# Running the two pairs of a triangular inverse in different rounds, with projection products between the steps

## The chip, the cores and the metric

The kernel runs on one core of a Trainium2 chip. TensorE does the matrix products and transpositions, VectorE (DVE), ScalarE (ACT) and GpSimd (POOL) the work around them, and SyncE (SP) issues most transfers. Each engine runs its own instructions strictly in order and waits on semaphores for the others. The metric is the device time of the whole kernel in microseconds: the median of several runs.

## The reference, cut to what matters

The program is two layers. The change touches the first, a gated delta rule over 8 sequences of 1024 steps with a 128x128 state each:

```python
q = x @ Wq + bq;  v = x @ Wv + bv;  gate = sigmoid(x @ Wg + bg)
kr = x @ Wk + bk; k = kr / max(norm(kr), 1e-12)
alpha = sigmoid(x @ Wa + ba);  beta = sigmoid(x @ Wb + bb)
# per step and sequence
Sk = S @ k_t
S  = a * (S - b * outer(Sk, k_t)) + b * outer(v_t, k_t)
o  = (q_t @ S) * g_t
x  = layernorm(x + o @ Wo + bo)
```

After it come a quantised MLP of six matrices with LoRA parts and a low rank MLP, each with a LayerNorm. Their code is the same in both kernels.

## The kernel before, in words

The 128 steps of a chunk are solved at once. Within a chunk the rule is a triangular system, so each chunk and sequence needs the inverse of a unit triangular 128x128 matrix. There are 8 chunks, and the 8 sequences go in two groups of four: 16 **rounds** of four sequences. A round belongs to one chunk and one group.

In a round, for the sequences s = 0 to 3: `xT.s` transposes the input (four 128x128 transpositions on TensorE, a rounded copy on ScalarE, the rest of the rounding on VectorE); `seed` writes the bias into a PSUM bank on ScalarE; `proj.s` is 12 products of 512 columns (four slices of the input, three products each, since every fp32 value is split in a high and a low part); `sq` and `copy` take q, k, v and the gate out on ScalarE. `ab`, `decay` and `A` make the decays of alpha and beta; `root` and `kh` norm k; `qkT` transposes q and k; `kk` multiplies k with itself; `MnT`, `M`, `W0` make the first state of the inverse.

The **levels** follow. The inverse is built by doubling: six levels, each for two **pairs** of sequences (pair 0 is s = 0, 1 and pair 1 is s = 2, 3). A level i of pair h is: `T.i.h` transposes the state (2 transpositions, then a copy on ScalarE into `Z_both`), `Y.i.h` multiplies it with M (then VectorE copies a masked part into `L`), `X.i.h` multiplies Z with L (then VectorE adds into the state `XZ`). The sixth ends in `inverse`. The chain of a level is TensorE, VectorE, TensorE, VectorE, and the next level of the same pair needs its end. The two pairs alternate, so one fills part of the other's waits.

With the inverse made, the round's second half runs a round later (a `'` in the order), mixed with the next round's first half: `KS`, `U`, `PT`, `O`, `S` compute the outputs and the new state, `ogT` and `attn.s` the output projection, and `z`, `stats`, `norm` the residual and LayerNorm. `''` is two rounds later.

The order is written out by hand, in the text `ORDER`, which the same function `run` reads for each engine: an engine takes from it the pieces in which it has work. The loop body holds two rounds. The last round has an order with more pieces (`MORE`, `ORDER_LAST`), among them the unpacking of the quantised weights (`dequant`) for the next layer, and `TAIL` follows. PSUM has eight banks, and the names `p_tr`, `p_pj`, `p_small`, `p_wide`, `p_pair` say which piece writes where.

## Time and profile before

| what | value |
|---|---|
| median of 3 runs | 2498.21 us (2495.07 to 2499.21) |
| profiled execution | 2494.1 us, its span 2492.3 us |
| busy over the span | PE 97%, DVE 67%, ACT 47%, POOL 27% |
| first layer's rounds | from 8.6 us to 722.5 us of the span |
| a round in the steady state | 43.2 us |

PE is TensorE, PEld its weight loads. A row of the timeline is a start, a duration, an engine, a line of the code, what is written and read, and in brackets how long the engine had been idle and for whom. A small product's duration is mostly latency: 128 columns take 0.27 us from start to end, but the next starts 0.11 us after it. So the busy share of PE says little about how full it is, and the distances between starts are used instead.

### The profile page before, as it was taken

The numbers are of one execution on the slowest core, as the hardware profiler recorded it, in microseconds if no ns is written. First come the engines' busy times: TensorE is split into PE (matmuls) and PEld (weight loads), VectorE is DVE, ScalarE is ACT, GpSimd is POOL, SyncE is SP. The second block draws the span as 40 slices with busy tenths as digits, with TensorE's granted clock in tenths as the row PEclk, the third lists the DMA queues.
The fourth block names the chain that finished last, engine by engine and source line by source line (L and its number), as shares of the span: only waits on it lengthen the run. The fifth ranks groups of instructions, "written<-read, shape, count | busy, mean of one in ns | idle before, by whom it ended". The sixth has DMA issues, their size and how long they took to land.

```text
span 2492.3 us, 37474 instructions
## 1 busy us (share of the span) xinstructions
...
## 2 busy tenths in 40 slices
...
GB/s 132 52 68 40 94 67 101 34 101 67 77 140 59 1 68 35 17 84 0 83 18 17 84 0 101 0 17 84 0 101 46 75 95 102 106 114 121 113 84 68
DMA packets 100655, 166.28 MB, mean 67 GB/s; under 512 B 18356, under 2 KB 21428, under 8 KB 100468
## 3 DMA queue, kind: packets, MB, share of 16 engines
...
q10 hardware_dynamic: 4036, 1.84, 0.3%
...
## 4 chain that ended last, share of the span: by engine, by line
PE 66%; DVE 1%; POOL 1%; issue 0%; ACT 0%; POOLq 0%; DVEq 0%
PE quant_bank L1436 7%; PE quant_bank L1438 7%; PE quant_bank L1437 7%; PE quant_bank L1826 6%; PE quant_bank L1828 6%; PE quant_bank L1827 6%; PE quant_bank L1463 5%; PE quant_bank L1464 5%; PE quant_bank L1465 5%; PE quant_bank L1453 3%; PE quant_bank L1482 2%; PE quant_bank L1484 2%; PE quant_bank L1483 2%; PE quant_bank L1843 1%; PE quant_bank L1494 1%; PE quant_bank L1425 1%
## 5 line engine op out<-in xcount | busy, mean ns | idle before, releaser
L1305 ACT ACTIVATE quant_g_hi<-quant_bank,kept_beta,kept_gamma 128x512 fp32r<-128x512 f32 x192 | 150.6, 784 | 395.6 <-PE quant_bank L1453 395.6
L1277 POOL TENSOR_SCALAR quant_var<-quant_mv 128x1 f32<-128x1 f32 x256 | 56.9, 222 | 1006.2 <-DVE quant_mv L1352 1006.2
L1436 PE MATMUL quant_bank<-kept_W_hi,quant_h_hi 128*128 128x512 f32 x768 | 305.4, 398 | 0.3 <-DVE quant_h_lo L1341 0.3
L1437 PE MATMUL quant_bank<-kept_W_lo,quant_h_hi 128*128 128x512 f32 x768 | 303.5, 395 | 0.0
L1438 PE MATMUL quant_bank<-kept_W_hi,quant_h_lo 128*128 128x512 f32 x768 | 303.4, 395 | 0.0
L1350 DVE BATCH_NORM_STATS2 quant_stats<-quant_bank 128x6 f32<-128x512 f32 x192 | 133.9, 698 | 196.4 <-PE quant_bank L1438 196.4
L1791 DVE TENSOR_TENSOR mlp_g_lo<-quant_bank,mlp_g_hi 128x512 fp32r<-128x512 f32 x256 | 176.4, 689 | 105.4 <-ACT quant_bank L1728 105.3
L1727 ACT ACTIVATE mlp_g_hi<-quant_bank,mlp_b 128x512 fp32r<-128x512 f32 x256 | 177.3, 693 | 70.7 <-PE quant_bank L1828 63.6
L1463 PE MATMUL quant_bank<-quant_g_hi,kept_W_hi 128*128 128x512 f32 x512 | 205.2, 401 | 0.0
L1464 PE MATMUL quant_bank<-quant_g_hi,kept_W_lo 128*128 128x512 f32 x512 | 202.5, 396 | 0.0
L1465 PE MATMUL quant_bank<-quant_g_lo,kept_W_hi 128*128 128x512 f32 x512 | 202.4, 395 | 0.0
L1372 DVE TENSOR_TENSOR quant_g_lo<-quant_bank,quant_g_hi 128x512 fp32r<-128x512 f32 x192 | 130.2, 689 | 100.4 <-ACT quant_bank L1306 98.2
L1320 ACT ACTIVATE quant_bank<-kept_b_all 128x512 f32<-128x512 f32 x192 | 113.3, 603 | 133.3 <-DVE quant_y L1365 74.7
L1438 PEld LDWEIGHTS quant_bank<-kept_W_hi,quant_h_lo 128*128 128x128 f32 x768 | 144.0, 187 | 35.1
L1436 PEld LDWEIGHTS quant_bank<-kept_W_hi,quant_h_hi 128*128 128x128 f32 x768 | 144.0, 188 | 34.6 <-issue 0.5
L1437 PEld LDWEIGHTS quant_bank<-kept_W_lo,quant_h_hi 128*128 128x128 f32 x768 | 144.1, 188 | 34.1
L1728 ACT ACTIVATE quant_bank<-quant_bank,mlp_b 128x512 f32<-128x512 f32 x256 | 168.3, 658 | 0.0
L1365 DVE TENSOR_SCALAR quant_y<-quant_bank,quant_mv,quant_rstd 128x512 f32<-128x512 f32 x192 | 155.5, 810 | 17.2 <-POOL quant_rstd L1279 17.2
L1279 POOL TENSOR_TENSOR quant_rstd<-quant_var,quant_minus_half 128x1 f32<-128x1 f32 x256 | 140.9, 550 | 21.3
L1306 ACT ACTIVATE quant_bank<-quant_bank,kept_beta,kept_gamma 128x512 f32<-128x512 f32 x192 | 145.4, 757 | 0.0
L1315 ACT ACTIVATE quant_h_hi<-kept_x_in 128x512 fp32r<-128x512 f32 x128 | 81.9, 640 | 123.6 <-DVE kept_x_in L1384 99.7
L1686 POOL TENSOR_SCALAR mlp_z<-mlp_z,mlp_mv,mlp_rstd 128x512 f32<-128x512 f32 x60 | 123.9, 2082 | 0.0
...
## 6 DMA issues: line engine op xcount, KB each, us to landing
...
```

Source lines behind the costliest of these rows:

```text
L1305: nc.scalar.activation(g_hi[m][:, k, :], tr[k][:, :], ACT.Gelu, bias=beta[:, b, k:k + 1], scale=gamma[:, b, k:k + 1])
L1365: nc.vector.tensor_scalar(y[m][:, e, :], lin_of["up", m, b, e][:, :], mv[m][:, e, 0:1], rstd[m][:, e:e + 1], ALU.subtract, ALU.mult).then_ ...
L1436: mm(out, x_hi, W_hi[2 * b][:, k, :], start=False, stop=False, skip_group_check=True)
L1437: mm(out, x_hi, W_lo[2 * b][:, k, :], start=False, stop=False, skip_group_check=True)
L1438: last = mm(out, x_lo, W_hi[2 * b][:, k, :], start=False, stop=k == KT - 1, skip_group_check=True)
L1463: mm(out, W_hi[2 * b + 1][:, k, cols], g_hi[m][:, k, :], start=k == 0, stop=False)
L1464: mm(out, W_lo[2 * b + 1][:, k, cols], g_hi[m][:, k, :], start=False, stop=False)
L1465: last = mm(out, W_hi[2 * b + 1][:, k, cols], g_lo[m][:, k, :], start=False, stop=k == KT - 1)
L1727: nc.scalar.activation(g_hi[:, at, :], p_h[at][:, :], ACT.Gelu_apprx_tanh, bias=b1[:, f:f + 1])
L1728: nc.scalar.activation(p_h[at][:, :], p_h[at][:, :], ACT.Gelu_apprx_tanh, bias=b1[:, f:f + 1]).then_inc(s_["gelu_done"], 1)
L1791: nc.vector.tensor_tensor(g_lo[:, at, :], p_h[at][:, :], as_f32(g_hi[:, at, :]), ALU.subtract).then_inc(s_["g_lo_done"], 1)
L1826: mm(out, lhs[0], rhs[0], start=first, stop=False)
```

## The change

The two pairs no longer alternate. Pair 0's levels stay at the end of the round, pair 1's move to the start of the next one, where they carry a `'`. Between the products of a level stand other pieces: the projections, cut into six parts each (`proj.s.0` to `proj.s.3` are two products, the high input against both parts of the weights; `proj.s.4` and `.5` are two products with the low input), and `xT`, `KS`, `PT`, `O`, `ogT`. `Y` now comes ahead of `T`. `seed` is a piece of its own. `S` is cut in four and the state update `Su` is put behind it; `PT` and `O` are cut in two and four. The state update and the four residual additions on GpSimd (`res`) get places of their own. Each pair gets its own semaphores and two banks in place of shared ones. In the last round pair 1's levels follow alone, since there is no next round, and the unpacking of the weights is spread over pair 0's levels. The number of products, transpositions and copies in a round is the same.

```diff
-        kk_halves = [p[:, 0:2 * P].rearrange("p (s n) -> p s n", s=2) for p in (p_small, p_tr[0])]
-
+        kk_halves = [p_tr[0][:, 0:2 * P].rearrange("p (s n) -> p s n", s=2)] * 2
+        YX_bank, T_bank = [p_tr[0], p_pair[1]], [p_tr[1], p_small]
...
-        Y_ps_of = [p_wide[:, 0:P], p_tr[1][:, 0:P]]
-        X_ps_of = [p[:, 0:P] for p in p_pair]
-        last_ps_of = [p[:, 0:P].rearrange("p (y n) -> p y n", y=2) for p in p_pair]
+        Y_ps_of = [p[:, 0:P] for p in YX_bank]
+        X_ps_of = [p[:, P:2 * P] for p in YX_bank]
+        last_ps_of = [p[:, 2 * P:3 * P].rearrange("p (y n) -> p y n", y=2) for p in YX_bank]
+        T_halves = [p[:, 0:2 * P].rearrange("p (s n) -> p s n", s=2) for p in T_bank]
...
         ORDER = order("""
-            bv.0' xT.0 xT.1 KS.0' proj.0 stats.0'' stats.1'' stats.2'' sq.0 copy.0 U.0' xT.2 proj.1 norm.0'' stats.3'' norm.1'' sq.1 copy.1 PT.0' xT.3 norm.2'' norm.3''
-            S.0' O.0' ab.0 root.0 proj.2 sq.2 copy.2 ogT.0' decay.0 kh.0
-            proj.3 sq.3 root.1 qkT.0 qkT.1 copy.3 attn.0' A.0 kh.1 kk.0 attn.1' MnT.0 qkT.2 qkT.3 qkA.0 z.0' M.0 W0.0 attn.2' z.1' kk.1 attn.3' MnT.1 M.1 W0.1
-            T.1.0 Y.1.0 T.1.1 Y.1.1 X.1.0 X.1.1
-            T.2.0 Y.2.0 T.2.1 Y.2.1 X.2.0 X.2.1
-            T.3.0 Y.3.0 T.3.1 Y.3.1 X.3.0 X.3.1
-            T.4.0 Y.4.0 T.4.1 Y.4.1 X.4.0 X.4.1
-            T.5.0 Y.5.0 T.5.1 Y.5.1 X.5.0 X.5.1
-            T.6.0 Y.6.0 T.6.1 Y.6.1 inverse.0 z.2' inverse.1 z.3'""")
+            bv.0' xT.0 seed.0 xT.1 seed.1
+            Y.1.1' T.1.1' proj.0.0 stats.0'' X.1.1' proj.0.1
+            Y.2.1' T.2.1' proj.0.2 stats.1'' X.2.1' proj.0.3 xT.2
+            Y.3.1' T.3.1' proj.0.4 norm.0'' X.3.1' proj.0.5 sq.0 copy.0 seed.2 stats.2''
+            Y.4.1' T.4.1' proj.1.0 norm.1'' X.4.1' proj.1.1 xT.3
+            Y.5.1' T.5.1' proj.1.2 stats.3'' X.5.1' KS.0'
+            Y.6.1' T.6.1' proj.1.3 norm.2'' inverse.1' proj.1.4 proj.1.5 sq.1 copy.1 seed.3
+            ab.0 norm.3'' root.0 U.0' proj.2.0 proj.2.1 decay.0 kh.0 proj.2.2 proj.2.3 S.0' S.1' qkT.0 qkT.1 A.0 S.2' kk.0 S.3' MnT.0 res.0' proj.2.4 proj.2.5 sq.2 copy.2 M.0 W0.0
+            Y.1.0 T.1.0 PT.0' X.1.0 PT.1'
+            Y.2.0 T.2.0 O.0' X.2.0 O.1' res.1'
+            Y.3.0 T.3.0 O.2' X.3.0 O.3' res.2'
+            Y.4.0 T.4.0 proj.3.0 X.4.0 proj.3.1 res.3'
+            Y.5.0 T.5.0 proj.3.2 Su.0' X.5.0 proj.3.3 Su.1'
+            Y.6.0 T.6.0 proj.3.4 Su.2' ogT.0' inverse.0 Su.3' proj.3.5 sq.3 copy.3 root.1
+            attn.0' kh.1 attn.1' z.0' qkT.2 attn.2' qkT.3 kk.1 attn.3' z.1' MnT.1 M.1 W0.1 z.2' z.3' qkA.0""")
...
+        MORE = {("KS", 0, 1): [("unit", 0, 0)] + dequants((0, 0)),
+                ("ab", 0, 0): dequants((0, 1), (0, 2), (0, 3)),
+                ("kh", 0, 0): dequants((1, 0), (1, 1)),
+                ("kh", 1, 0): [("bv", 0, 0)]}
+        for i, tiles in enumerate(([(1, 2)], [(1, 3)], [(2, 0)], [(2, 1)], [(2, 2), (2, 3)])):
+            MORE["X", (i + 1, 0), 0] = dequants(*tiles)
...
+        for i in range(1, LEVELS - 1):
+            ORDER_LAST += [("Y", (i, 1), 0), ("T", (i, 1), 0)]
+            if i < 5:
+                ORDER_LAST += [("stats", i - 1, 1)]
+            ORDER_LAST += [("X", (i, 1), 0)]
+            if i > 1:
+                ORDER_LAST += [("la_hi", i - 2, 0), ("norm", i - 2, 1)]
+        ORDER_LAST += [("Y", (LEVELS - 1, 1), 0), ("T", (LEVELS - 1, 1), 0), ("lb_hi", 0, 0), ("inverse", 1, 0), ("lb_hi", 1, 0), ("lb_hi", 2, 0)]
...
-                seed(c, g, s)
...
+            def proj(c, g, at):
+
+                s, part = at
+                n = GROUPS * c + g
+                if part == 0:
+                    if isinstance(n, int) and n == s == 0:
+                        pe.wait_ge(s_["w_lo_done"], 2)
+                    pe.wait_ge(s_["xT_hi_done"], GB * n + s + 1)
+                    pe.wait_ge(s_["seeded"], GB * n + s + 1)
+                if part == KT:
+                    pe.wait_ge(s_["xT_lo_done"], GB * n + s + 1)
                 out, cols = p_pj[s % 2][:, :], slice(0, PROJ)
-                for k in range(KT):
-                    mm(out, xT_hi[:, s, k, :], w_hi[:, k, cols], start=False, stop=False, skip_group_check=True)
-                    mm(out, xT_hi[:, s, k, :], w_lo[:, k, cols], start=False, stop=False, skip_group_check=True)
-                pe.wait_ge(s_["xT_lo_done"], GB * n + s + 1)
-                for k in range(KT):
-                    last = mm(out, xT_lo[:, s, k, :], w_hi[:, k, cols], start=False, stop=k == KT - 1, skip_group_check=True)
-                last.then_inc(s_["proj_ps"], 1)
+                if part < KT:
+                    mm(out, xT_hi[:, s, part, :], w_hi[:, part, cols], start=False, stop=False, skip_group_check=True)
+                    mm(out, xT_hi[:, s, part, :], w_lo[:, part, cols], start=False, stop=False, skip_group_check=True)
+                else:
+                    for k in (2 * (part - KT), 2 * (part - KT) + 1):
+                        last = mm(out, xT_lo[:, s, k, :], w_hi[:, k, cols], start=False, stop=k == KT - 1, skip_group_check=True)
+                    if part == KT + 1:
+                        last.then_inc(s_["proj_ps"], 1)
...
+            def PT_(c, g, h):
+
+                if h == 1:
+                    dve.wait_ge(s_["PT_ps"], GROUPS * c + g + 1)
+                    nc.vector.tensor_tensor(PT[:, :, :], wide, DT[g][:, :, :], ALU.mult).then_inc(s_["PT_done"], 1)
...
+            def Su(c, g, s):
+
+                n = GROUPS * c + g
+                if s == 0:
+                    dve.wait_ge(s_["O_ps"], n + 1)
+                dve.wait_ge(s_["S_ps"], 2 * n + s // 2 + 1)
+                nc.vector.scalar_tensor_tensor(S[g][:, s, :, :], S[g][:, s, :, :], A[g][:, s, P - 1:P], pair[s // 2][:, s % 2, :, :],
+                                               ALU.mult, ALU.add).then_inc(s_["S_done"], 1)
...
+                if s == 2:
+                    pe.wait_ge(s_["inverse_done"], 2 * n + 1)
...
+                nc.tensor.transpose(T_halves[h][:, 1, :], MnT[:, 2 * h + 1, :], ident).then_inc(s_["M_ps"], 1)
```

TensorE, one level in the steady state, in the order of the kernel before (both pairs; p_small and p_wide are pair 0's banks, p_tr pair 1's):

```order
L923 MATMUL delta_p_small<-kept_ident_61,delta_XZ_114 128x128
L924 MATMUL delta_p_small<-kept_ident_61,delta_XZ_114 128x128
L933 MATMUL delta_p_wide<-delta_XZ_114,delta_M_both 128x128
L923 MATMUL delta_p_tr<-kept_ident_61,delta_XZ_114 128x128
L924 MATMUL delta_p_tr<-kept_ident_61,delta_XZ_114 128x128
L933 MATMUL delta_p_tr<-delta_XZ_114,delta_M_both 128x128
L941 MATMUL delta_p_pair<-delta_L_81,delta_Z_both 128x128 x2
```

and in the changed order, the second level of pair 1 (L956 is Y, L944 and L945 are T, L859 and L860 projection products, L964 is X, L843 transposes the input of the third sequence):

```order
L956 MATMUL delta_p_pair<-delta_XZ_114,delta_M_both 128x128
L944 MATMUL delta_p_small<-kept_ident_61,delta_XZ_114 128x128
L945 MATMUL delta_p_small<-kept_ident_61,delta_XZ_114 128x128
L859 MATMUL delta_p_pj<-delta_w_hi,delta_xT_hi 128x512
L860 MATMUL delta_p_pj<-delta_w_lo,delta_xT_hi 128x512
L962 REGISTER_ALU
L964 MATMUL delta_p_pair<-delta_L_79,delta_Z_both 128x128
L859 MATMUL delta_p_pj<-delta_w_hi,delta_xT_hi 128x512
L860 MATMUL delta_p_pj<-delta_w_lo,delta_xT_hi 128x512
L843 MATMUL delta_p_tr<-kept_ident_61,delta_x_in_110 128x128 x4
```

The other pair's products are gone from the level, and products of a projection stand in both gaps.

TensorE, from the last projection's end on, before (L889 is qkT of the first two sequences, L1017 to L1019 attn, L897 is kk):

```order
L845 MATMUL delta_p_pj<-delta_w_hi,delta_xT_lo 128x512 x4
L889 MATMUL delta_p_tr<-kept_ident_61,delta_qkv 128x128
L889 MATMUL delta_p_tr<-kept_ident_61,delta_kb 128x128
L889 MATMUL delta_p_tr<-kept_ident_61,delta_khat_69 128x128
L889 MATMUL delta_p_tr<-kept_ident_61,delta_qkv 128x128
L889 MATMUL delta_p_tr<-kept_ident_61,delta_kb 128x128
L889 MATMUL delta_p_tr<-kept_ident_61,delta_khat_69 128x128
L1017 MATMUL delta_p_pj<-delta_wo_hi,delta_ogT_hi 128x512
L1018 MATMUL delta_p_pj<-delta_wo_lo,delta_ogT_hi 128x512
L1019 MATMUL delta_p_pj<-delta_wo_hi,delta_ogT_lo 128x512
L897 MATMUL delta_p_small<-delta_qkT_75 128x128 x2
```

and now (L1051 to L1053 attn, L910 qkT of the third sequence):

```order
L863 MATMUL delta_p_pj<-delta_w_hi,delta_xT_lo 128x512 x2
L1051 MATMUL delta_p_pj<-delta_wo_hi,delta_ogT_hi 128x512
L1052 MATMUL delta_p_pj<-delta_wo_lo,delta_ogT_hi 128x512
L1053 MATMUL delta_p_pj<-delta_wo_hi,delta_ogT_lo 128x512
L1051 MATMUL delta_p_pj<-delta_wo_hi,delta_ogT_hi 128x512
L1052 MATMUL delta_p_pj<-delta_wo_lo,delta_ogT_hi 128x512
L1053 MATMUL delta_p_pj<-delta_wo_hi,delta_ogT_lo 128x512
L910 MATMUL delta_p_tr<-kept_ident_61,delta_qkv 128x128
L910 MATMUL delta_p_tr<-kept_ident_61,delta_kb 128x128
L910 MATMUL delta_p_tr<-kept_ident_61,delta_khat_103 128x128
L1051 MATMUL delta_p_pj<-delta_wo_hi,delta_ogT_hi 128x512
L1052 MATMUL delta_p_pj<-delta_wo_lo,delta_ogT_hi 128x512
```

The transpositions of the first two sequences have left the place between the last projection and attn, and two attn stand ahead of the third sequence's.

VectorE, from the second pair's first state on, before (L704 to L708 are W0, L714 the masked copies of both pairs' first level, L720 the addition):

```order
L704 COPY_PREDICATED delta_XZ_76<-delta_mask_both,delta_MnT 128x64
L706 COPY_PREDICATED delta_XZ_76<-delta_mask_both,delta_p_tr 128x64
L708 TENSOR_TENSOR delta_M_both<-delta_p_pair,delta_MnT 128x128
L39 ISA
L714 COPY_PREDICATED delta_L_78<-delta_mask_both,delta_p_wide 128x128
L39 REGISTER_ALU
L714 COPY_PREDICATED delta_L_78<-delta_mask_both,delta_p_tr 128x128
```

and now (L713 and L715 are W0, L781 is z, L685 bv, L644 the low part of xT, L721 the masked copy of pair 1's first level):

```order
L713 COPY_PREDICATED delta_XZ_76<-delta_mask_both,delta_p_small 128x64
L715 TENSOR_TENSOR delta_M_both<-delta_p_small,delta_MnT 128x128
L780 REGISTER_ALU
L781 TENSOR_TENSOR delta_z<-delta_p_pj,delta_x_res_123 128x512 x2
L685 TENSOR_TENSOR delta_bv_70<-delta_qkv,delta_ab 128x512
L643 ISA
L644 TENSOR_TENSOR delta_xT_lo<-delta_p_tr,delta_xT_hi 128x512
L643 REGISTER_ALU
L644 TENSOR_TENSOR delta_xT_lo<-delta_p_tr,delta_xT_hi 128x512
L721 COPY_PREDICATED delta_L_78<-delta_mask_both,delta_p_pair 128x128
```

Two z, bv and two low parts now stand between the first state and the first level's copy.

## Rows read from the trace of the kernel before

**Rows 1.** Stages: us, busy and instructions per engine, TensorE clock, DMA share, GB/s

```profile
405.70:448.87 43.17, 41.97 (x262) 34.39 (x262) 30.32 (x73) 16.25 (x46) 13.06 (x19) 1.00 0.28 97
435.94:448.87 12.93, 11.73 (x78) 9.43 (x77) 7.61 (x27) 3.54 (x12) 2.49 (x4) 1.00 0.00 0
```

**Rows 2.** Timeline of one level: start, us, engine, line, what; idle before in brackets

```profile
401.41 0.28 PE L923 MATMUL delta_p_small<-kept_ident,delta_XZ 128*128 128x128 f32 x1
401.64 0.39 PE L933 MATMUL delta_p_wide<-delta_XZ,delta_M_both 128*128 128x128 f32 x2
401.84 0.28 ACT L596 ACTIVATE delta_Z_both<-delta_p_small 128x128 f32<-128x128 f32 x1 [1.19 <-PE delta_p_small L924]
402.13 0.30 DVE L714 COPY_PREDICATED delta_L<-delta_mask_both,delta_p_wide 128x128 f32<-128x128 int32 x1 [0.23 <-PE delta_p_wide L933]
...
402.57 1.05 PE L941 MATMUL delta_p_pair<-delta_L,delta_Z_both 128*128 128x128 f32 x4
...
403.07 0.29 DVE L720 TENSOR_TENSOR delta_XZ<-delta_p_pair,delta_XZ 128x128 f32<-128x128 f32 x1
403.46 0.28 PE L923 MATMUL delta_p_small<-kept_ident,delta_XZ 128*128 128x128 f32 x1
```

**Rows 3.** Timeline: first projection, then U's eight products

```profile
407.57 0.47 PE L841 MATMUL delta_p_pj<-delta_w_hi,delta_xT_hi 128*128 128x512 f32 x1
...
410.43 0.28 PE L967 MATMUL delta_p_pair<-delta_XZ,delta_bR 128*128 128x128 f32 x1
...
411.32 0.28 PE L970 MATMUL delta_p_pair<-delta_bR,delta_XZ 128*128 128x128 f32 x1
```

**Rows 4.** Timeline: from the last projection to the third transposition of q and k

```profile
429.99 0.28 ACT L558 ACTIVATE delta_sq<-delta_p_pj 128x128 f32<-128x128 f32 x1 [3.36 <-PE delta_p_pj L845]
...
431.77 0.43 DVE L667 TENSOR_TENSOR delta_kb<-delta_qkv,delta_rnb 128x256 f32<-128x256 f32 x1
...
432.60 0.32 PE L889 MATMUL delta_p_tr<-kept_ident,delta_qkv 128*128 128x128 f32 x1
```

**Rows 5.** Timeline: second pair, from the product of k to its first state

```profile
434.13 2.38 POOL L494 TENSOR_TENSOR delta_qkA<-delta_qkT,delta_A 128x1024 f32<-128x1024 f32 x1 [2.52 <-ACT delta_qkT L584]
...
435.56 1.11 DVE L704 COPY_PREDICATED delta_XZ<-delta_mask_both,delta_MnT 128x64 f32<-128x64 int32 x1
...
436.52 0.30 DVE L706 COPY_PREDICATED delta_XZ<-delta_mask_both,delta_p_tr 128x64 f32<-128x64 int32 x1
```

**Rows 6.** Timeline: ScalarE and VectorE at a round's start

```profile
406.34 0.60 ACT L550 ACTIVATE delta_xT_hi<-delta_p_tr 128x512 fp32r<-128x512 f32 x1 [1.47 <-PE delta_p_tr L829]
...
406.40 0.68 DVE L767 TENSOR_TENSOR delta_z<-delta_p_pj,delta_x_res 128x512 f32<-128x512 f32 x1
...
406.83 0.60 ACT L545 ACTIVATE delta_p_pj<-delta_b_all 128x512 f32<-128x512 f32 x1
...
407.00 0.68 DVE L678 TENSOR_TENSOR delta_bv<-delta_qkv,delta_ab 128x512 f32<-128x512 f32 x1
```

**Rows 7.** Timeline: one LayerNorm statistic

```profile
409.40 0.69 DVE L772 BATCH_NORM_STATS2 delta_stats<-delta_z 128x6 f32<-128x512 f32 x1
```

**Rows 8.** Timeline: ScalarE behind a finished projection, first and last

```profile
415.64 0.28 ACT L558 ACTIVATE delta_sq<-delta_p_pj 128x128 f32<-128x128 f32 x1 [1.70 <-PE delta_p_pj L845]
...
416.28 0.28 ACT L563 ACTIVATE delta_gate<-delta_p_pj 128x128 f32<-128x128 f32 x1
```

**Rows 9.** Timeline: the products for alpha and beta, and their last sigmoid

```profile
420.26 0.48 PE L855 MATMUL delta_p_tr<-delta_xT_hi,delta_w_ab 128*34 128x512 f32 x1
...
424.36 0.70 ACT L571 ACTIVATE delta_a_rest<-delta_ab_sum,delta_b_ab 2x508 f32<-2x508 f32 x1
```

**Rows 10.** First round, a thinly filled stretch: columns as in rows 1

```profile
42.00:44.00 2.00, 0.89 (x7) 0.64 (x6) 2.00 (x5) 0.76 (x2) 0.00 (x0) 1.00 0.00 0
44.00:46.00 2.00, 1.43 (x7) 1.14 (x8) 1.24 (x5) 0.11 (x1) 1.81 (x1) 0.59 0.00 0
```

**Rows 11.** Last round, a stretch of waits: columns as in rows 1

```profile
690.00:700.00 10.00, 4.48 (x15) 3.44 (x14) 6.22 (x12) 0.60 (x3) 1.80 (x4) 0.67 0.86 279
```

169 lines of the change are left out of this document (78 added, 91 removed).

## The prediction

> **What bounds the kernel now.** I read the summary of engines first, then the stages of one round, then the timeline of a level and of the places where pieces change their neighbours. The change touches only the first layer, 16 rounds, so everything is worked out per round. A steady round takes 43.17 us, with VectorE busy for 30.32 us of it and ScalarE for 16.25 [rows 1]. The levels are its last 12.93 us. PE shows 11.73 us busy there, but that counts latency. By starts it is less full: a level of both pairs repeats every 2.05 us (401.41 to 403.46) [rows 2]. A small product or transposition issues every 0.11 us, so a level needs 4 transpositions (0.44), 2 Y and 2 X of two passes each (0.89), 1.33 us. Five levels and the sixth thus leave TensorE about 4.4 us without work per round. Outside the levels I find about 1 us. So TensorE's own work is about 38 us a round, and the prize is at most 5 us a round, 80 us in all. The bound inside the levels is a chain through three engines, outside it TensorE.
>
> **One pair alone.** With Y ahead of T, and from the handoffs of rows 2: Y at 0; T issues at 0.22; the copy on ScalarE starts 0.43 later (401.41 to 401.84) and takes 0.28; X starts 0.14 after a finished input (402.43 to 402.57), so at 1.07. The masked copy of Y starts at 0.49 (401.64 to 402.13) and ends at 0.79, so it is not late. The addition starts 0.50 after X (402.57 to 403.07), takes 0.29, and the next Y comes 0.10 later (403.36 to 403.46). Sum 1.96 us for **one** pair, against 2.05 for both before. The sixth level ends in two longer product groups, about 1.7. Two pairs: 10 x 1.96 + 2 x 1.7 = 23.0 us of chain, 10.1 more than 12.93.
>
> **What moves into it.** A projection takes 2.86 us of TensorE (407.57 to 410.43), a part 0.47; eight passes of 128 columns take 0.89 (410.43 to 411.32) [rows 3]. Into the gaps go proj.0 (2.86), four parts of proj.1 (1.9), five of proj.3 (2.4), KS and PT (0.89 each), O (1.78), xT.2 and xT.3 (0.44 each), ogT (0.44): 12.0 us. Were nothing else late, the round would be 43.2 + 10.1 - 12.0 = 41.3 us. That is 1.9 less than now, not the 5 of the prize, since a level has 1.30 us free and gets 0.94 to 1.4. What follows is what else becomes late. I worked it out by putting the pieces on the five engines in the new order with the durations of the rows.
>
> **The stretch from the last projection to pair 1's first X.** TensorE work in it: four attn (2.8), qkT.2 and .3 (0.66), kk.1 (0.45), M.1 (0.22), xT.0 and .1 (0.88), Y, T and a part (0.9), 5.9 us. The waits, one by one:
> a. attn.0' needs the low part of ogT: two operations of 0.60 and 0.69 us behind ogT, which stands just ahead of the end of the chain: 0.65.
> b. qkT.2 needs kh.1. From the square of the last projection to it the trace shows 2.61 us (429.99 to 432.60) [rows 4], through ScalarE, VectorE, GpSimd and back. Before, qkT.0, qkT.1, kk.0 and two attn covered this. Now two attn do (1.4 us), and the first VectorE step queues behind ogT_lo, an addition and a state update (0.9 more): 1.45.
> c. attn.2' needs z.0', which is queued behind kh.1 on VectorE: 0.35.
> d. kk.1 stands directly behind qkT.3 and waits for its copy on ScalarE: 0.8.
> e. The first state (W0.1) has a copy that starts at 435.56 and takes 1.11 us, and the next one, of 0.30, starts at 436.52, when the 2.38 us of GpSimd's qkA (from 434.13) end [rows 5]. qkA still starts with qkT.3's copy, so W0.1 ends no sooner, and Y.1.1' with it. xT.0 and xT.1 cover 0.9 of it, 0.6 is left. The Trainium skill says that GpSimd's memory interface is shared with VectorE and contended where VectorE has two SBUF inputs (GPSIMD Engine Reference, 1. Specifications); this trace agrees, and by that rule the residual additions, which now stand behind kh.0, could hold up W0.0 as well.
> f. The largest: before pair 1's first masked copy VectorE has z.2', z.3', bv, and the low parts of xT.0 and xT.1 to do. Such operations follow one another every 0.6 us (406.40 to 407.00) [rows 6], 3.0 us from W0.1's end. ScalarE's copy of T stands behind two high parts and two seeds, 0.5 us each (406.34 to 406.83), and ends before the masked copy does. So X.1.1' starts 3.4 us after Y.1.1' and not 1.07: 2.35.
> Sum 6.2 us, where the same pieces cost about 0.8 now: +5.4.
>
> **Pair 1's levels.** In level 3 the high and low part of xT.2 run ahead of the masked copy, and in level 5 those of xT.3: transpose, 0.3, ScalarE 0.60, VectorE 0.68, then the copy, so X is late by 0.9 each. In level 4 ScalarE does sq, copy, gate and seed of the first projection ahead of T's copy: 0.92 from sq to the gate's end (415.64 to 416.56) [rows 8], and 0.5 for the seed, started only when proj.0.5 has ended: X late by 0.9. The gaps of levels 2, 4 and 5 get more (1.11 to 1.13 us with X) than the 0.89 that the chain has there: 0.7. A statistic of 0.69 us and its follower stand ahead of the additions of levels 1 and 2 [rows 7], and KS's subtraction ahead of the sixth copy: 0.3. Sum 3.7.
>
> **Between the pairs.** From ab's first product to the end of the last sigmoid it is 4.8 us (420.26 to 425.06) [rows 9]. Then decay, a scan, kh.0, qkT, kk.0, MnT.0 and W0.0 follow in a chain, 13.0 us to Y.1.0 by the same handoffs. It holds 11.0 us of TensorE's work (ab 1.84, U 1.78, proj.2 2.86, decay 1.4, S 1.78, the rest 1.3). So 2.0 of waits, against about 0.5 now: +1.5.
> **Pair 0's levels.** PT's product on VectorE must end before O.0' may start, and og and Su stand ahead of copies: +0.4.
>
> Sum of a round: 41.3 + 5.4 + 3.7 + 1.5 + 0.4 = 52.3 us.
>
> **The clock.** In the first round TensorE was busy for 0.89 of 2 us, and in the next 2 us the granted clock was 0.59 on average [rows 10]: it fell from 2.4 to 1.2 GHz behind a stretch that was less than half filled. The wait f is such a stretch: in the 3.4 us from Y.1.1' to X.1.1' 0.9 us of work is issued. The work of the one or two levels behind it (1.3 to 1.6 us each) then issues at half rate, but partly in gaps of the chain. No row prices it: 0 at least, and up to 3 us a round. I take 0.7, nearer to nothing, since the steady rounds of rows 1, waits included, show a granted clock of 1.00. Round: 53.0 us, 9.8 more than now.
>
> **The ends.** Pair 1's levels of the last round run alone at the end: 5 x 1.96 + 1.7 = 11.5 us more. Against that, the last round waits today: in 690 to 700 us there is little work and the clock is low [rows 11], because six dequants that need late loads stand ahead of the chain. Now three of them do, and the others lie between the levels. That gives back 6 to 9 us, and the statistics and norms that come out of the tail some 3 more. The first round gains and loses alike. I count the ends at 0, within +-6.
>
> 15 rounds x 9.8 = +147 us on the profiled 2494.1 is 2641. The runs' median stands 4 us above the profiled execution: **2645 us**. With half of each contention term the round is 47 and the time 2555. With the clock's upper end it is 55.5 and 2680, with the waits a tenth longer 2695. Its own range is 2560 to 2700.
>
> **Rivals.**
> 1. *The chain covers what I count as late, faster.* If the VectorE queue at a round's start and ScalarE's block in level 4 ran inside waits that pair 1 has anyway, the round were 41.3 + about 0.8 of stalls, 42.1: 2498 - 15 x 1.1 - 6 = 2475 us. For it speaks that VectorE has 12.85 us of idle time a round and ScalarE 27. Against it: they work in order, and the pieces stand ahead of the level's copy in the new order, so idle time behind them doesn't help. It decides when a, b and f together are under 1 us; I find 4.5. 0.10, with 0.02 more for no difference.
> 2. *Half covered.* The overlaps of neighbouring operations hide more than I count, because durations contain latency: round 46, 2540 us. 0.12.
> 3. *The clock stays down.* If the stretches of waits b to f keep TensorE at 1.2 GHz into pair 1's levels, then some 7 us of products issue at half rate: +7 a round, 2645 + 15 x 6.3 = 2740 us. 0.08. The Trainium skill tells of kernels whose clock falls anew in each waiting gap and is paid for each time (TensorE: Matmul & The Clock Gate, HAM oscillation). By that rule this would be the likely case; the steady round here shows a granted clock of 1.00, and only the first and last rounds bear the rule out.
>
> **Chances.** The forecast 0.68, rival 2 0.12, rival 3 0.08, rival 1 0.12 with the tie. A measurement of this kernel tells 0.2% (5 us) from no change. Faster 0.10, same 0.02, slower 0.88. The range 2550 to 2700 leaves out the faster case, part of rival 2 and most of rival 3.
>
> **What would show it.** Rounds 53 us apart by the starts of xT.0. VectorE's z and bv rows directly ahead of pair 1's first masked copy, and X.1.1' 3 to 3.5 us behind Y.1.1' (f). About 1.5 us of idle TensorE ahead of qkT.2, waiting for khat (b). In pair 1's third, fourth and fifth level X about 2 us after Y, in the others 1.1. Pair 0's levels 1.95 to 2.1 us apart. A granted clock below 1 at the round's start, if the clock's term is real. It would be wrong if the rounds are 42 us apart with a full TensorE, or if one pair's level takes less than 1.8 us.

## The result: slower by 7.0%

| kernel | median | ratio to before, 95% interval | span of the profiled execution |
|---|---|---|---|
| before | 2496.93 us | | 2492.3 us |
| changed | 2671.64 us | 1.0702 [1.0687, 1.0717] | 2669.0 us |

The prediction was 2645 us with a range of 2550 to 2700. The time lies in the range, 27 us above the value named.

The profile page of the changed kernel, its busy shares and granted clock (tenths, 40 slices):

```profile
PE 2463.2 (92%) x12383; PEld 1956.2 (73%) x12383; DVE 1688.8 (63%) x3181; ACT 1173.2 (44%) x2225; POOL 670.6 (25%) x1090
PEclk7999999999999899999999999999999999999999
```

The profiled execution takes 177 us more for the same work and every share is lower: time went into waits. Stretches of the changed kernel, columns as in [rows 1]:

```profile
390.42:445.33 54.91, 45.11 (x263) 33.74 (x261) 31.31 (x73) 16.50 (x46) 13.59 (x20) 0.97 0.22 76
449.78:465.69 15.91, 13.39 (x73) 10.36 (x73) 9.26 (x25) 3.90 (x12) 3.22 (x8) 0.91 0.00 0
885.00:900.00 15.00, 10.13 (x37) 6.71 (x37) 10.05 (x26) 2.78 (x8) 6.95 (x10) 0.66 0.35 56
```

The first is a whole steady round (xT.0 to xT.0), which answers to the first line of [rows 1]: 54.9 us for 43.17, with 45.1 us of TensorE busy for 42.0, since latency and a lower clock count as busy. The mean of 14 rounds is 54.50 us against 43.22. The second reaches from X.1.1' to ab's first product and holds the rest of pair 1's levels; the third is the end of the last round, where pair 1's levels stand alone.

**Wait f, the largest.** Timeline of the changed kernel from pair 1's first Y to its first X:

```profile
446.36 1.27 DVE L781 TENSOR_TENSOR delta_z<-delta_p_pj,delta_x_res 128x512 f32<-128x512 f32 x2
447.55 0.68 DVE L685 TENSOR_TENSOR delta_bv<-delta_qkv,delta_ab 128x512 f32<-128x512 f32 x1
448.15 1.28 DVE L644 TENSOR_TENSOR delta_xT_lo<-delta_p_tr,delta_xT_hi 128x512 fp32r<-128x512 f32 x2
446.68 0.50 PE L956 MATMUL delta_p_pair<-delta_XZ,delta_M_both 128*128 128x128 f32 x2 [0.26 <-DVE delta_M_both L715]
449.35 0.29 DVE L721 COPY_PREDICATED delta_L<-delta_mask_both,delta_p_pair 128x128 f32<-128x128 int32 x1
449.78 0.55 PE L964 MATMUL delta_p_pair<-delta_L,delta_Z_both 128*128 128x128 f32 x1 [1.26 <-DVE delta_L L721]
```

Y starts at 446.68, X at 449.78, 3.10 us later. By the handoff of [rows 2] the masked copy that X needs (L721) could start 0.49 us behind Y, yet five operations stand ahead of it on VectorE, and it starts 2.67 us behind. X follows its end.

**The clock behind it.** Windows of 2 us of the changed kernel:

```profile
448.00:450.00 2.00, 0.74 (x3) 0.33 (x3) 2.00 (x5) 0.86 (x3) 0.00 (x0) 0.83 0.00 0
450.00:452.00 2.00, 2.00 (x9) 1.75 (x9) 0.76 (x4) 0.00 (x0) 0.75 (x2) 0.50 0.00 0
452.00:454.00 2.00, 2.00 (x13) 1.64 (x12) 1.30 (x4) 0.28 (x1) 0.73 (x2) 0.81 0.00 0
```

TensorE is busy for 0.74 of 2 us, and then it runs at 1.2 GHz (0.50), as in [rows 10]. By windows of 1 us the granted clock is 0.67 from 449 to 450, 0.50 to 452, 0.63 to 453 and 1.00 from there on.

**Where the sum was short.** VectorE and GpSimd of the changed kernel between the pairs, and the first transposition of q and k:

```profile
418.58 0.90 DVE L674 TENSOR_TENSOR delta_kb<-delta_qkv,delta_rnb 128x256 f32<-128x256 f32 x1
419.40 1.48 DVE L675 TENSOR_TENSOR delta_khat<-delta_qkv,delta_rn 128x256 f32<-128x256 f32 x1
416.69 5.33 POOL L520 TENSOR_TENSOR delta_x_res<-delta_x_res,delta_bo_all 128x512 f32<-128x512 f32 x4
421.01 0.32 PE L910 MATMUL delta_p_tr<-kept_ident,delta_qkv 128*128 128x128 f32 x1 [1.66 <-DVE delta_khat L675]
```

In [rows 4] kb takes 0.43 us. Here it takes 0.90 and khat 1.48, beside four residual additions on GpSimd, and TensorE waits 1.66 us for khat.

### The profile page after: what moved, and what is told of

Its sections match the earlier page's. It is cut to its first block, busy times and chain, and to the rows that moved or that the text cites. A ratio compares the mean times of both kernels' runs of the same rounds, so it can differ in the third digit from the quotient of the medians.

```text
span 2669.0 us, 37347 instructions
## 1 busy us (share of the span) xinstructions
PE 2463.2 (92%) x12383; PEld 1956.2 (73%) x12383; DVE 1688.8 (63%) x3181; ACT 1173.2 (44%) x2225; POOL 670.6 (25%) x1090
## 4 chain that ended last, share of the span: by engine, by line
PE 62%; DVE 1%; POOL 1%; issue 0%; ACT 0%; POOLq 0%; DVEq 0%
PE quant_bank L1472 6%; PE quant_bank L1471 6%; PE quant_bank L1470 6%; PE quant_bank L1862 5%; PE quant_bank L1860 5%; PE quant_bank L1861 5%; PE quant_bank L1497 4%; PE quant_bank L1498 4%; PE quant_bank L1499 4%; PE quant_bank L1487 3%; PE quant_bank L1516 2%; PE quant_bank L1518 2%; PE quant_bank L1517 2%; PE quant_bank L1459 1%; PE quant_bank L1877 1%; PE quant_bank L1528 1%
## 5 line engine op out<-in xcount | busy, mean ns | idle before, releaser
L859 PE MATMUL delta_p_pj<-delta_w_hi,delta_xT_hi 128*128 128x512 f32 x256 | 126.9, 496 | 16.6 <-DVE delta_wo_lo L637 9.5
```

## The experiments

Rounds are compared in five stages by starts on TensorE, each the mean of eight steady rounds (in the changed kernel those whose Y.1.1' starts at 337.3 to 719.6 us), in us: **1** from Y.1.1' to X.1.1'; **2** to the transposition of alpha and beta (L886), which holds the rest of pair 1's levels, the first two projections, KS, ab, U and the start of the third projection; **3** to Y.1.0, which holds decay, S, qkT of pair 0 and the rest of it; **4** pair 0's levels, to the first product of attn.0'; **5** to the next Y.1.1'.

| run | 1 | 2 | 3 | 4 | 5 | round | median, us |
|---|---|---|---|---|---|---|---|
| changed | 3.17 | 20.56 | 9.83 | 13.08 | 7.98 | 54.62 | 2671.6 |
| res_gate | 3.17 | 20.60 | 8.05 | 13.09 | 7.99 | 52.90 | 2645.2 |
| lo_gap | 2.31 | 18.20 | 9.64 | 13.09 | 7.98 | 51.22 | 2621.0 |
| z_early | 2.19 | 19.88 | 9.82 | 13.09 | 7.99 | 52.96 | 2647.9 |
| seed_early | 3.17 | 19.37 | 10.82 | 13.08 | 7.98 | 54.43 | 2668.8 |
| warm | 3.17 | 19.87 | 9.62 | 13.08 | 7.98 | 53.72 | 2660.1 |
| fill_out | 3.17 | 20.98 | 10.99 | 14.66 | 8.22 | 58.01 | 2723.1 |
| a_qka | 4.17 | 21.18 | 10.02 | 13.08 | 7.51 | 55.96 | 2689.7 |
| all_four | 1.63 | 17.49 | 8.05 | 13.07 | 7.99 | 48.24 | 2575.8 |
| all_five | 1.85 | 17.49 | 8.06 | 13.08 | 7.77 | 48.25 | 2574.5 |

In kernels whose clock falls in some rounds and not in others, another choice of eight rounds moves the mean of a round by 0.2 us (0.4 in a_qka). So stages are also compared between single rounds. In the changed kernel six of the eight rounds have 20.8 us in stage 2 and 9.6 in stage 3, one has 19.9 and 11.2, one 19.8 and 9.6. The first kind has a fall of the clock in stage 2, the second in stage 3, the last none.

**1. Hold GpSimd's residual additions (res_gate).**

```diff
+                n = GROUPS * c + g
                 if s == 0:
                     pool.wait_ge(x_res_dma[g], 16 * c + 16)
+                    if not isinstance(n, int) or n < GROUPS * CHUNKS - 1:
+                        pool.wait_ge(s_["W0_done"], 2 * n + 3)
```

> The changed kernel with one wait more: GpSimd's four residual additions of 5.33 us each, which in the changed kernel start at 416.69 of the trace, right behind the reciprocal of the norm and nearly 3 us ahead of the vector work on kb and khat, now start only when pair 0's first state of the round is done. Main theory (the additions slow the vector work that makes TensorE wait for qkT.0: kb took 0.90 us where the kernel before has 0.43, khat 1.48 against 0.42): those two rows fall back to under 0.6 us, the stretch from ab to Y.1.0 shrinks from 14.5 us to about 13.0, and the kernel gains 1.5 to 2 us in each of 15 rounds, about 22 us of 2672, to some 2650. Rival (the stretch is set by the scan of the decay and the reciprocal, whatever GpSimd does): the rows may shrink, the time stays within 4 us. A second rival (the additions only move onto VectorE's copies in pair 0's levels and slow these): time within 4 us or worse, with longer states in the levels.

Ratio to before 1.0598 [1.0580, 1.0615], 26 us less. The timeline of this run:

```profile
410.39 0.40 DVE L677 TENSOR_TENSOR delta_kb<-delta_qkv,delta_rnb 128x256 f32<-128x256 f32 x1
410.70 0.42 DVE L678 TENSOR_TENSOR delta_khat<-delta_qkv,delta_rn 128x256 f32<-128x256 f32 x1
415.54 4.96 POOL L523 TENSOR_TENSOR delta_x_res<-delta_x_res,delta_bo_all 128x512 f32<-128x512 f32 x4 [6.99 <-DVE delta_XZ L716]
```

The two rows fall back to 0.40 and 0.42 us, TensorE no longer sits idle ahead of qkT.0, and stage 3 is 1.78 us shorter in the mean, 1.6 between rounds with a full clock there (9.63 to 8.05): the main theory holds. Pair 0's levels do not suffer from the additions that now run beside them (stage 4 the same). The mean of stage 2 is the same too, but it hides two kinds of rounds in turn, 21.35 us with a fall of the clock and 19.85 without. The thin stretch ahead of the two is alike (windows of two successive rounds, ahead of X.1.1' and behind it):

```profile
386.00:388.00 2.00, 0.73 (x3) 0.33 (x4) 2.00 (x5) 0.91 (x3) 0.00 (x0) 1.00 0.00 0
390.00:392.00 2.00, 2.00 (x14) 1.59 (x14) 0.70 (x4) 0.70 (x2) 0.75 (x2) 1.00 0.00 0
438.00:440.00 2.00, 0.70 (x2) 0.31 (x3) 2.00 (x5) 1.11 (x3) 0.00 (x0) 1.00 0.00 0
442.00:444.00 2.00, 2.00 (x8) 1.46 (x7) 1.07 (x4) 0.28 (x1) 0.75 (x2) 0.50 0.00 0
```

**2. The low part of xT into the gaps (lo_gap).** VectorE's `xT` pieces become `lo` pieces; `lo.0` goes behind the copy of Y in level 1, `lo.1`, `lo.2`, `lo.3` likewise in levels 2, 4 and 6. The statistics and norms that stood at these places go behind the copy of X or of the inverse:

```diff
-            Y.1.1' T.1.1' proj.0.0 stats.0'' X.1.1' proj.0.1
+            Y.1.1' T.1.1' proj.0.0 lo.0 X.1.1' proj.0.1 stats.0''
...
-            Y.4.1' T.4.1' proj.1.0 norm.1'' X.4.1' proj.1.1 xT.3
+            Y.4.1' T.4.1' proj.1.0 lo.2 X.4.1' proj.1.1 xT.3 norm.1''
```

> The changed kernel with VectorE's order altered: the low part of the transposed input (1.27 us) is a piece of its own, put behind the copy of Y in levels 1, 2, 4 and 6 of pair 1, where TensorE runs products that don't wait for VectorE, and the statistics and norm that stood there go behind the copy of X. Nothing is added or left out. Main theory (the odd levels of pair 1 take 1.9 us because a 1.28 us piece of VectorE stands ahead of the copy of Y, and the first product of X waits 3.1 us behind Y for the same queue): level 1's wait falls by 1.2 us, the lone slow levels by up to 0.9 us each, in sum 2 to 3 us per round, 30 to 45 us of 2672, to 2627 to 2642. Rival (the levels are set by the one-pair chain of TensorE, ScalarE and VectorE, the queue pieces fit beside it): within 0.2%, 2666 to 2678. Second rival (the pieces now stand ahead of the copies of X instead and cost as much there): within 0.2% or slower.

1.0506 [1.0489, 1.0524], 51 us less where 30 to 45 were expected. Level 3 of this run, and the same level of the changed kernel:

```profile
429.85 0.68 DVE L786 BATCH_NORM_STATS2 delta_stats<-delta_z 128x6 f32<-128x512 f32 x1
430.34 0.39 PE L956 MATMUL delta_p_pair<-delta_XZ,delta_M_both 128*128 128x128 f32 x2
430.83 0.31 DVE L721 COPY_PREDICATED delta_L<-delta_mask_both,delta_p_pair 128x128 f32<-128x128 int32 x1
431.36 0.38 PE L964 MATMUL delta_p_pair<-delta_L,delta_Z_both 128*128 128x128 f32 x1
```

```profile
453.96 0.39 PE L956 MATMUL delta_p_pair<-delta_XZ,delta_M_both 128*128 128x128 f32 x2
454.80 0.69 DVE L644 TENSOR_TENSOR delta_xT_lo<-delta_p_tr,delta_xT_hi 128x512 fp32r<-128x512 f32 x1 [1.25 <-ACT delta_xT_hi L558]
455.40 0.29 DVE L721 COPY_PREDICATED delta_L<-delta_mask_both,delta_p_pair 128x128 f32<-128x128 int32 x1
455.84 0.46 PE L964 MATMUL delta_p_pair<-delta_L,delta_Z_both 128*128 128x128 f32 x2 [0.81 <-DVE delta_L L721]
```

From Y to X it is 1.02 us without the low part ahead of the copy and 1.88 with it, in level 5 likewise. In this run a statistic of the same length (0.68 us) stands ahead of the copy in level 3 and costs nothing, since its input is ready and it starts ahead of Y. The low part has to wait 1.25 us for ScalarE's high part first, and the copy behind it waits too. Stage 1 falls by 0.86, and stage 2 by 2.36, of which 0.7 is the clock (run 5): in this run it stays at 1.00 from 424 to 432 us. Level 4 stays at 1.91 us.

**3. The z products earlier (z_early).**

```diff
-            attn.0' kh.1 attn.1' z.0' qkT.2 attn.2' qkT.3 kk.1 attn.3' z.1' MnT.1 M.1 W0.1 z.2' z.3' qkA.0""")
+            attn.0' kh.1 attn.1' z.0' qkT.2 attn.2' qkT.3 kk.1 attn.3' z.1' z.2' MnT.1 M.1 z.3' W0.1 qkA.0""")
```

> The changed kernel with three of TensorE's and VectorE's pieces of the last round in another order: the second z product of the pair ahead of M.1, the last one ahead of W0.1. Nothing is added or left out. Main theory (in the changed kernel the last z copies stand behind the first state of pair 1 on VectorE, at 446.36 of the trace, and the product X.1.1' waits for the queue until 449.78): the queue is 1.1 us shorter there, the kernel gains about 1.1 us in each of 15 rounds, 16 us, to about 2655. Rival (that place waits for the chain through GpSimd's product of the masks and its addition, not for z): within 0.2%.

1.0615 [1.0597, 1.0633], 24 us less where 16 were expected. Stage 1 falls by 0.98 where 1.1 was worked out. Stage 2 falls by 0.68 too, and the windows behind X.1.1' (437.50) show why:

```profile
436.00:438.00 2.00, 1.16 (x6) 0.73 (x6) 1.94 (x4) 1.00 (x3) 0.00 (x0) 1.00 0.00 0
438.00:440.00 2.00, 1.92 (x11) 1.16 (x10) 1.31 (x4) 0.28 (x1) 0.75 (x2) 1.00 0.00 0
```

With the wait one microsecond shorter, TensorE is busy for 1.16 of 2 us and the clock does not fall here, in none of the eight rounds. (In this one it falls later, in stage 3.)

**4. The seed of the first projection later (seed_early).** On ScalarE `sq.0 copy.0 seed.2` go from behind X.3.1' to behind its copy of T.4.1'.

> The changed kernel with the square, copy and seed of the first projection's norm issued one level later than its last product, behind T.4.1' in place of behind X.3.1'. Nothing is added or left out. Main theory (ScalarE's work on the projection stands ahead of its copy of T in pair 1's levels 3 and 4 and makes these levels 1.9 us long instead of about 1.1 over their products): 0.9 us per round less, about 13 us of 2672, to about 2659. Rival (that level's length is VectorE's 1.28 us piece alone): within 0.2%. Second rival (the projection's memory is freed later and TensorE waits for it at proj.1.0): slower by up to 1 us per round, 15 us.

1.0694 [1.0677, 1.0712], 3 us less than the changed kernel: by the total, the rival. By the stages it is neither. Stage 2 is 1.2 us shorter, and stage 3 is 1.0 longer. The eight rounds are of two kinds: in six, stage 3 takes 11.2 us, in two 9.6. Windows of one of the six, behind the wait for khat:

```profile
420.00:422.00 2.00, 0.71 (x7) 0.52 (x5) 2.00 (x3) 0.00 (x0) 2.00 (x3) 1.00 0.92 262
424.00:426.00 2.00, 2.00 (x9) 2.00 (x10) 0.60 (x2) 0.00 (x0) 0.00 (x0) 0.50 1.05 401
```

The clock falls at this second thin place, while behind X.1.1' it stayed high in seven of the eight rounds (stage 2 at 19.2 us). Of the changed kernel's eight rounds, one shows 11.2 in stage 3, and its stage 2 has 19.9 where six of the others have 20.8. The level's own gain (20.8 less the clock's 0.9 to 19.2, about 0.65) was eaten by the clock. Why the fall moves to the later place is not shown.

**5. Fill wait f (warm).** Five products of 512 columns behind proj.0.0, their results unused.

```diff
-            Y.1.1' T.1.1' proj.0.0 stats.0'' X.1.1' proj.0.1
+            Y.1.1' T.1.1' proj.0.0 warm.0 stats.0'' X.1.1' proj.0.1
...
+            def warm(c, g, _):
+                for _ in range(5):
+                    mm(p_wide[:, :], xT_hi[:, 0, 0, :], w_hi[:, 0, 0:PROJ], start=True, stop=True)
```

> The changed kernel with five products of 512 columns more on TensorE in each round, behind the first projection's first bank in level 1 of pair 1, where TensorE otherwise waits about 3 us for X.1.1'; their results are not used. Main theory (behind that wait the granted clock of TensorE falls to 0.50 for two windows of 2 us, at 450 and beside it, and the projection's products there run at half rate): the products fill the wait, the clock stays high, the fill of level 1 runs in about 2.2 us in place of 3.06, and the kernel gains 0.8 us per round, 12 us of 2672, to about 2660. Rival (the fall is caused by all waits between the levels together, one filled wait is not enough): the clock row is as before and the time within 0.2%. Second rival (five products of about 0.43 us each are over 2 us that the wait does not wholly cover because the products are issued before VectorE's pieces end): slower by up to 1 us per round, 15 us.

1.0658 [1.0641, 1.0675], 12 us less, with more work done. The windows of this run at the place (X.1.1' at 449.48):

```profile
448.00:450.00 2.00, 1.89 (x9) 1.27 (x9) 1.92 (x4) 0.56 (x2) 0.00 (x0) 1.00 0.00 0
450.00:452.00 2.00, 1.91 (x11) 1.17 (x10) 1.30 (x4) 0.28 (x1) 0.75 (x2) 1.00 0.00 0
```

Stage 1 is what it was, stage 2 shorter by 0.7 and stage 3 by 0.2: in none of the eight rounds does the clock fall. This prices the falls by themselves: 0.9 us a round in the mean. By single rounds, one in stage 2 costs 0.9 us (20.8 against 19.9) and one in stage 3 costs 1.6 (11.2 against 9.6).

**6. Take the pieces out again (fill_out).** proj.3 goes from between the products of pair 0's levels 4 to 6 to a place behind them.

> The changed kernel with the six products groups of the fourth projection (proj.3.0 to proj.3.5) wholly behind the levels of pair 0 and not between their products. Nothing is added or left out. Theory (a piece moved between the products of a level is free as long as it fits in the level's wait, and pair 0's levels 4 to 6 take about 2 us with their pieces but would take 1.1 to 1.3 us less without them): TensorE's products of this projection, some 5 us, come to stand by themselves while three levels fall from about 2.0 to 1.1 or 1.3 us; net 2.4 us per round more, 36 us, to about 2708. Rival (the pieces make the levels as much longer as they take, nothing is hidden): within 0.2% of 2672. Second rival (the levels do not get shorter because the handoffs set them at 1.9 us): the whole 5 us per round is added, 75 us, to about 2747.

1.0909 [1.0892, 1.0925], 51 us more than the changed kernel, 3.4 a round, where 36 were expected. Level 5 of this run, without pieces, up to the Y of level 6:

```profile
516.06 0.49 PE L956 MATMUL delta_p_tr<-delta_XZ,delta_M_both 128*128 128x128 f32 x2 [0.38 <-DVE delta_XZ L727]
517.14 0.49 PE L964 MATMUL delta_p_tr<-delta_L,delta_Z_both 128*128 128x128 f32 x2 [0.37 <-ACT delta_Z_both L603]
518.01 0.49 PE L956 MATMUL delta_p_tr<-delta_XZ,delta_M_both 128*128 128x128 f32 x2 [0.39 <-DVE delta_XZ L727]
```

The same two Y in the changed kernel, with four products of proj.3 between them:

```profile
433.55 0.49 PE L956 MATMUL delta_p_tr<-delta_XZ,delta_M_both 128*128 128x128 f32 x2
435.49 0.49 PE L956 MATMUL delta_p_tr<-delta_XZ,delta_M_both 128*128 128x128 f32 x2
```

And two windows of this run, in stage 4 of the round shown and in stage 3 of the round ahead of it:

```profile
519.00:521.00 2.00, 2.00 (x9) 1.88 (x8) 1.00 (x3) 0.78 (x2) 0.00 (x0) 0.50 0.00 0
448.00:450.00 2.00, 2.00 (x8) 1.77 (x8) 0.73 (x2) 0.00 (x0) 0.00 (x0) 0.50 1.05 389
```

The level takes 1.95 us with nothing in its gaps, and 1.94 in the changed kernel with products in them: the pieces there cost nothing, and the chain sets the level. The expected fall to 1.1 to 1.3 us was wrong; the second rival has the mechanism, but not its 5 us. The clock falls twice in each of the eight rounds. One fall is in stage 2. The other is in stage 3 in seven of them (11.2 us), and stage 4 then takes 14.5, 1.4 more than in the changed kernel, since the twelve products also cover the wait for ogT's low part. In the round shown it comes in stage 4, where four of the products issue at half rate, and the stage takes 15.8. In the mean stage 4 grows by 1.6 us, stage 3 by 1.2, stage 2 by 0.4 and stage 5 by 0.2. Why moving this projection makes the clock fall a second time in every round was not tried.

**7. Hold qkA behind the first state, changed kernel (a_qka).**

```diff
+                pool.wait_ge(s_["W0_done"], 2 * n + 2)
```

> The changed kernel with one wait more: GpSimd's product qkA of 2.4 us starts only when pair 1's first state is done; in the changed kernel it runs from 443.65 to 446.01 beside VectorE's predicated copies, the first of which takes 1.27 us at 444.90 where its fellows alone take 0.30. Nothing is added or left out. Theory (both engines slow each other while their operands come from SBUF, and this copy stands on the way from MnT.1 to X.1.1'): the copy falls to 0.3 us and TensorE's X.1.1' comes 0.75 us earlier, 11 us over 15 rounds, and as the wait ahead of X.1.1' is shorter, the clock behind it stays high too, worth 0.8 us more per round as in the run with z ahead (24 us measured for 16 worked out): 2648 to 2660. Rival (the slow stretch only moves onto VectorE's product bv or the copies of z that stand behind it in the queue, so X.1.1' comes when it came): within 0.2% of 2671. Second rival (qkA held back delays what needs it, the product A times V of the next stretch): slower.

1.0781 [1.0765, 1.0798], **18 us more**. Only the second rival had the sign, and for another reason. The timeline of this run, GpSimd last:

```profile
455.86 0.30 DVE L712 COPY_PREDICATED delta_XZ<-delta_mask_both,delta_MnT 128x64 f32<-128x64 int32 x1
456.70 1.28 DVE L782 TENSOR_TENSOR delta_z<-delta_p_pj,delta_x_res 128x512 f32<-128x512 f32 x2
457.89 1.85 DVE L686 TENSOR_TENSOR delta_bv<-delta_qkv,delta_ab 128x512 f32<-128x512 f32 x1
459.67 1.28 DVE L645 TENSOR_TENSOR delta_xT_lo<-delta_p_tr,delta_xT_hi 128x512 fp32r<-128x512 f32 x2
456.83 2.37 POOL L505 TENSOR_TENSOR delta_qkA<-delta_qkT,delta_A 128x1024 f32<-128x1024 f32 x1 [5.69 <-DVE delta_XZ L714]
```

The copy L712 is short as expected and stage 5 gains 0.47. But bv, from 0.68 us, takes 1.85 as the rival said, in the very queue that sets stage 1 (+1.00), and stage 2 is 0.6 longer: the clock falls there in each of the eight rounds, for six of eight in the changed kernel. The rival had taken the loss to be no larger than the gain. The copy is 0.97 us shorter and only 0.47 of that shows; bv is 1.17 longer, and 1.00 of that shows.

**8, 9. Four edits, and five (all_four, all_five).** Runs 1 to 4 together; with run 7's as the fifth.

> The changed kernel with four edits of order and wait together: the residual additions held until pair 0's first state, the low part of xT in the gaps of pair 1's levels, the z products ahead of M.1 and W0.1, and the seed of the first projection one level later. The four alone gave 26, 51, 24 and 3 us. Main theory (they stand at different places, three of four terms add up): about 100 us of 2672, to 2570, 3% slower than the kernel before still, since the chain of twelve one-pair levels stays. Rival (the low part of xT and the z copies shorten the same wait ahead of X.1.1', which is then set by something else): only the larger of the two counts there, about 80 us, 2590. The opposite rival (the main loss was the queue and not the chain, TensorE's clock recovers once the waits are short): 2520 or less.

> The changed kernel with the four edits of the run all_four (2576 us) and GpSimd's product qkA held until pair 1's first state. Nothing is added or left out. Theory (the slow predicated copy of 1.27 us stands on the way from MnT.1 to Y.1.1' and X.1.1' there too): 0.5 to 0.75 us less per round, 8 to 11 us, to about 2566. Rival (after the other edits the wait there is already short and the product only slows what now follows): within 0.2% of 2576.

All four: 1.0322 [1.0306, 1.0337], 96 us less than the changed kernel; the single gains add up to 104. That these come so close is chance in part, since by stages they do not add up: in stage 2 the single gains make 4.2 us a round and together they give 3.1, for the fall of the clock that each of runs 2 to 4 removes is counted more than once; in stage 3 they make 1.0 and together give 1.8, for the loss of run 4 there is gone. A round takes 48.2 us at a clock of 1.00:

```profile
401.99:450.21 48.22, 43.92 (x260) 32.60 (x261) 28.95 (x73) 16.38 (x46) 12.84 (x20) 1.00 0.13 43
```

With the fifth, 1.0321 [1.0305, 1.0336]: no difference. Stage 1 loses the 0.22 us that stage 5 gains. The rival had it: in all_four the masked copy takes 0.52 us already, since qkA ends sooner after the copy's start, so only 0.22 was left to gain.

Over 14 rounds all_four has 48.27 us a round. So 6.2 of the 11.3 us came from the order of pieces and the additions' place, and 5.05 are left. They are not all shown to be the price of the one-pair levels: TensorE is idle for 4.30 us of the round shown (48.22 less 43.92), against 1.20 in the first line of [rows 1], and 2.0 of it stand ahead of attn.0', qkT.2 and kk.1 (waits a, b and d of the prediction), which no run touched.

**10 to 12. The kernel before, with parts of this (b_yfirst, b_qka, b_both).** In b_yfirst each level reads `Y.i.0 T.i.0 Y.i.1 T.i.1` for `T.i.0 Y.i.0 T.i.1 Y.i.1`, and T of level 1 waits for M_both as in the changed kernel; b_qka has run 7's line.

> The kernel before with one thread of the change alone: in each level, Y is issued ahead of T for both pairs, as in the changed kernel, with the levels of the two pairs still side by side. Nothing is added or left out. Theory (VectorE's copy of Y with its predicated copy is the longer of the two ways through the level, X waits for it, Y issued first brings it forward by about 0.09 us per level): 0.4 to 0.5 us per round, 7 us of 2495, to about 2488. Rival (X waits for ScalarE's copy of T, which now comes later by the same 0.09 us or more): 7 us slower. Second rival (both ways end together): within 0.2%, 2490 to 2500.

> The kernel before with the same one wait: GpSimd's product qkA starts only when the second pair's first state is done; in the kernel before it starts at 434.13 and VectorE's first predicated copy at 435.56 takes 1.11 us beside it, the one at 436.52 not. Nothing is added or left out. Theory (this copy stands on the way to the second pair's first level, the levels start 0.5 to 0.8 us earlier): 8 us of 2495, to about 2487. Rival (the product then runs beside VectorE's copies in level 1 and slows these as much): within 0.2%. Second rival (what needs qkA comes late): slower.

> The kernel before with both: Y ahead of T in each level (alone 2488.8 against 2495.1, a gain of 6.3 us), and qkA held until the second pair's first state. Nothing is added or left out. Theory (the two act at different places, within the levels and ahead of them): 6 and 8 us add up to 14, to about 2481, faster than both kernels. Rival (qkA held back is worth nothing or lies on the copies of level 1): 2489 or more.

| run | median | ratio to before, 95% interval | round |
|---|---|---|---|
| before, beside these runs | 2494.8 us | | 43.2 us |
| b_yfirst | 2488.8 us | 0.9975 [0.9965, 0.9984] | 42.79 us |
| b_qka | 2489.8 us | 0.9980 [0.9971, 0.9989] | 42.9 us |
| b_both | 2484.1 us | 0.9956 [0.9942, 0.9969] | 42.5 us |

Y first gains 6 us where 7 were expected. qkA held gains 5 of 8: the masked copy takes 0.31 us where [rows 5] has 1.11 (timeline of b_qka):

```profile
431.55 0.31 DVE L705 COPY_PREDICATED delta_XZ<-delta_mask_both,delta_MnT 128x64 f32<-128x64 int32 x1
432.69 2.35 POOL L495 TENSOR_TENSOR delta_qkA<-delta_qkT,delta_A 128x1024 f32<-128x1024 f32 x1 [5.08 <-DVE delta_XZ L707]
```

Here bv does not stand behind the copy (it runs at the next round's start, [rows 6]), and the same line helps that hurt in run 7. Both together gain the sum, 11 us (14 were expected), and b_both is faster than both kernels, by 0.4% against the kernel before.

## Why the prediction came out where it did

**The sum.** Predicted +9.8 us a round, +147; measured +11.3 a round, +169 over 15, and +7 at the ends, 177 us of span. The 1.5 us a round that are missing are one term, the stretch between the pairs.

**The chain and its filling: right.** One-pair levels of 1.96 us were forecast; pair 0's stand 1.94 to 2.16 apart. Run 6 shows for levels 4 and 5 of pair 0 that they last as long with nothing in them, so pieces there are free, as the 12.0 us moved in were counted. Pair 0's levels (+0.4) fit too: from Y.1.0 to attn.0' the forecast's parts (five levels of 1.96, the sixth of 1.7, a part of 0.47, wait a of 0.65, and 0.4) give 13.0 us, and stage 4 has 13.08.

**From the last projection to X.1.1' (+5.4): right, a little high.** 12.1 us were worked out (5.9 of work and 6.2 of waits), 11.9 measured: the last product of proj.3.5 has issued by 437.85, and X.1.1' starts at 449.78. Wait f: 3.10 us for 3.4, and runs 2 and 3 confirm the VectorE queue as its cause by shortening it by 0.86 and 0.98. In the timeline TensorE is idle for 0.58 us ahead of attn.0' (a), 0.86 ahead of qkT.2 for khat (b, forecast 1.45), 0.58 ahead of kk.1 (d), 0.26 ahead of Y.1.1' (e); each is 0.16 more when counted from where the next product could have issued (a duration of 0.27 us against a spacing of 0.11). Wait c leaves no idle time; attn.2' starts 0.42 us behind the last transposition of qkT.2, so it is at most 0.3.

**Pair 1's levels (+3.7): right.** X.1.1' to ab's first product took 15.9 us in a round with a fall of the clock and 15.0 in one without; the forecast's parts give 15.0 without it. Levels 3, 4 and 5 take 1.88, 1.91 and 1.87 us from Y to X. Run 2 shows xT's low part as the cause in levels 3 and 5. Level 4 stayed at 1.91 there. Its X waits for ScalarE's copy:

```profile
458.60 0.49 PE L964 MATMUL delta_p_pair<-delta_L,delta_Z_both 128*128 128x128 f32 x2 [0.74 <-ACT delta_Z_both L603]
```

Run 4 points to the projection's work on ScalarE by a gain of about 0.65 that only a correction for the clock brings out.

**Between the pairs (+1.5): the term that was mis-sized.** From ab's first product to Y.1.0 (411.00 to 425.50) it is 14.5 us, 13.0 forecast; in run 1 it is 12.9, 1.6 less. The prediction had the residual additions "now stand behind kh.0" and able to hold up W0.0. They stand behind kh.0 only in the written order: on GpSimd nothing gates them once rnb is done, and VectorE gets to kb almost 2 us later. They lengthen kb and khat, not W0.0, and the prediction gave them no price. So the term is 3.0, not 1.5.

**The clock (+0.7): right in place; the size was luck.** Run 5 gives 0.9 us a round, 0.7 of it at the place that was named. But 0.7 was a choice between 0 and 3 that no row priced, and the forecast does not have the falls in stage 3. Rival 3, a clock that stays down, did not come: the clock is at 1.00 again from 453 us.

**The ends (0, within +-6): +7.** The first round takes 4.6 us and the last 19.0 more than before, the rest of the program 4.9 less, against the 11.3 that the fifteenth round was counted at. In the last round pair 1's lone levels run at a low clock (0.66 in the mean from 885 to 900 us, shown above, 0.50 from 891 to 901). The first takes 2.41 us and the next four 2.77 each, not the 1.96 that the sum had at full clock, 3.7 us in all. What the spread unpacking gave back was not measured, so the rest of the 7 is open.

**Rivals 1 and 2** fail by the stages: the VectorE queue was waited for almost in full (3.10 us for 3.4). With the faults of the terms (-0.2 for the stretch to X.1.1', +1.5 between the pairs, +0.2 for the clock) the sum of 53.0 comes to the measured 54.5.
